# Position terms sent in two halves, local values in three parts, latents batch by batch, contexts normalised early: one change to a fused decoder layer

## What is computed

```
n  = layernorm(x)
x1 = x + local_attention(n)             # 8 heads of 16, blocks of 12 tokens, context 24, a relative
                                        # position term shifted row by row, tanh cap at 50, softmax
x2 = x1 + cross_attention(layernorm(x1), ctx)
                                        # 16 heads of 64, 512 contexts per batch; both inputs get
                                        # their own layernorm inside; rope on the keys;
                                        # clip(q.k/8, -11, 11), softmax; @ Wo + bo
x3 = x2 + routed_mixture(layernorm(x2)) # 12 experts, top 3 of 12, three routers, gelu
```

## Time and profile before

| | |
|---|---|
| median of 3 runs | 504.03 us (503.49 to 505.67) |
| the profiled execution | 503.41 us |
| its span in the profile | 501.7 us |
| mean granted TensorE clock | 0.962 |
| PE busy | 450.8 us (90%) |
| PE weight loads | 327.8 us (65%) |
| DVE busy | 321.8 us (64%) |
| POOL busy | 241.8 us (48%) |
| ACT busy | 187.4 us (37%) |

### The profile page before, as it was taken

The page is one execution under the profiler, slowest core; times in us unless marked ns, Lnnn a source line. Parts: engine busy times, 40 slices in busy tenths (PEclk is TensorE's granted clock), DMA queues, the critical chain, the costliest instruction groups (busy, mean ns, idle before and its releaser), DMA issues.

```text
span 501.7 us, 8554 instructions
## 1 busy us (share of the span) xinstructions
PE 450.8 (90%) x3282; PEld 327.8 (65%) x3282; DVE 321.8 (64%) x686; ACT 187.4 (37%) x290; POOL 241.8 (48%) x209
## 2 busy tenths in 40 slices
PE   2982968988799999999999999588999999999997
PEld 1761746656466676667677667266667777888885
DVE  8952695999976756765769866834463533275454
ACT  5744435454444545543544544112334532300000
POOL 7441344789577776787678748224333333000000
PEclk9997887999899999999999999788999999999999
DMA  7359500000000000000000020010222110000000
GB/s 171 116 104 99 130 2 1 2 0 1 0 1 1 2 1 1 1 1 0 1 2 2 2 87 1 21 43 22 65 63 64 63 64 21 2 6 12 10 5 12
DMA packets 31658, 15.08 MB, mean 30 GB/s; under 512 B 16077, under 2 KB 29314, under 8 KB 31618
## 3 DMA queue, kind: packets, MB, share of 16 engines
q1 hardware_dynamic: 30916, 14.25, 12.3%
q10 hardware_dynamic: 702, 0.28, 0.2%
HBM read 12.56 MB, written 1.97 MB: 29 GB/s over the span
## 4 chain that ended last, share of the span: by engine, by line
PE 70%; DVE 16%; issue 4%; ACT 4%; DMA 3%; POOL 2%; SPq 1%; DVEq 0%; ACTq 0%; POOLq 0%
PE psum L1044 9%; PE psum L1027 9%; PE psum L847 7%; PE psum L1175 5%; PE psum L1212 4%; PE psum L1211 4%; PE psum L1213 4%; PE psum L1177 4%; PE psum L1176 4%; DVE xn L1255 3%; PE psum L1063 3%; PE psum L950 2%; PE psum L1078 2%; PE psum L1054 2%; DVE rden L1428 2%
## 5 line engine op out<-in xcount | busy, mean ns | idle before, releaser
L465 POOL TENSOR_TENSOR e_part<-e_sb 128x512 f32<-128x512 f32 x64 | 91.0, 1439 | 39.8 <-DVE e_sb L1421 39.8
L703 ACT ACTIVATE e_sb<-psum 128x1024 f32<-128x1024 f32 x64 | 62.2, 1023 | 15.6 <-PE psum L1027 15.5
L1027 PE MATMUL psum<-q_t,kT 64*128 64x256 f32 x512 | 64.8, 392 | 0.3 <-ACT e_sb L703 0.3
L1044 PE MATMUL psum<-e_sb,v_sb 128*64 128x256 f32 x512 | 63.7, 392 | 0.0
L497 POOL TENSOR_TENSOR xeT_lo<-xeT,xeT_hi 128x512 fp32r<-128x512 f32 x24 | 30.9, 1290 | 67.0 <-ACT xeT_hi L717 67.0
L1428 DVE RECIPROCAL rden<-psum 128x256 f32<-128x256 f32 x32 | 56.0, 1749 | 2.1 <-PE psum L1054 2.0
L457 POOL TENSOR_TENSOR k_rot<-rope_a,rope_b 128x512 f32<-128x512 f32 x32 | 41.3, 1291 | 32.8 <-DVE rope_b L1317 32.8
L1596 DVE SCALAR_TENSOR_TENSOR x_sb<-psum,dw,x_sb 128x128 f32<-128x128 f32 x96 | 33.7, 351 | 34.8 <-PE psum L1213 32.2
L685 ACT ACTIVATE kT<-psum 128x512 f32<-128x512 f32 x32 | 19.2, 599 | 94.5 <-PE psum L950 94.3
L1027 PEld LDWEIGHTS psum<-q_t,kT 64*128 64x128 f32 x512 | 47.3, 188 | 10.9 <-issue 5.2
L1421 DVE TENSOR_SCALAR e_sb<-e_sb 128x1024 f32<-128x1024 f32 x64 | 47.7, 781 | 7.5 <-ACT e_sb L703 7.5
(11 more groups left out here) (189 smaller groups left out, 793.2 us busy)
## 6 DMA issues: line engine op xcount, KB each, us to landing
w_raw<-in_L_ffn_W_dram SPq DMA_DIRECT2D x24, 256.0 KB, 2.7
ctx_sb<-in_ctx_dram SPq DMA_DIRECT2D x4, 256.0 KB, 5.7
bd_dram<-bd_raw SPq DMA_DIRECT2D x4, 206.2 KB
bd<-bd_dram SPq DMA_DIRECT2D x8, 99.0 KB
vbd<-v_dram SPq DMA_DIRECT2D x8, 79.7 KB
v_dram<-v_tok SPq DMA_DIRECT2D x4, 136.0 KB, 2.2
vbd<-v_dram SPq DMA_DIRECT2D x8, 65.3 KB
raw<-in_L_xattn_Wkv_dram SPq DMA_DIRECT2D x2, 256.0 KB, 5.4
```

Of the source, the lines that this page charges most:

```text
L465: pool.tensor_tensor(e_part[:, p % 2, half, :, :], e_sb[:, i % ERING, :, 0, :], e_sb[:, i % ERING, :, 1, :], ALU.add)\
L703: act.activation(e_sb[:, i % ERING, :, :, :].rearrange("p a k t -> p (a k t)"), psum[:, a:a + 2, :].rearrange("p a b -> p (a b)"), ACT.Exp ...
L1027: mm = pe.matmul(psum[:, 2 * (i % 2) + a, t * S:(t + 1) * S], kT[rows, p % 3, kt * P:(kt + 1) * P], q_t[rows, j % 2, p % 2, :], start=True ...
L1044: mm = pe.matmul(psum[DX * a:DX * a + DX, pv_bank(p), 0:S], v_sb[g % 2][:, kt, 2 * pp + a, :], e_sb[:, i % ERING, a, t, :], start=(kt == 0 ...
```

## The change

It has five parts.

1. **Position terms in two halves.** Chunks 0 to 2 (12 groups) and 3 to 5 (10 groups) are stored and loaded apart, each with semaphores of its own (4 + 4 stores, 8 + 8 loads). The third `relative` and `positions_out` stand ahead of the values; the store of the first half stands ahead of the stores of the values. `add_positions(c)` waits for its half alone.
2. **Values in three parts**: 24 DMAs of 33, 33 and 25 windows in place of 16 of 50 and 41. `local_values(c)` waits for its third.
3. **Contexts early.** On DVE the statistics of context batches 1 to 3 stand between the two halves of `add_positions`, and the normalisation of all three behind the second half, ahead of `local_normalize(0)`. The four last `weight_rest` of POOL stand behind their reciprocal deviations, and the two loads of Wq ahead of the context loads.
4. **Latents batch by batch**, 2 tiles at a time: batch 0 between the chunks of the local attention, batches 1, 2 and 3 in rounds 0 to 3, 6 to 9 and 14 to 17. `output_bias` moves from rounds 0 and 4 to rounds 5 and 18.
5. **The way into the rounds.** `turn_latents(0)` and `queries(0)` stand earlier on PE; one key unit and one `turn_keys` move behind the first scores.

The diff, cut to its core:

```diff
+        def spread_slots(part):
+            def slot(w):
+                return NBP * (w // NB) + w % NB
+            per = CG * WG * NCH // SPREADS
+            return slice(slot(per * part), slot(min(per * (part + 1), WALL) - 1) + 1)
+        def half_groups(half):
+            return slice(CG * HCH * half, min(CG * HCH * (half + 1), NGRP))
         def last_chunk(b):
...
-        LATENT_ROUNDS = (1, 2, 3)
+        LATENT_ROUNDS = {1: (0, 1, 2), 2: (6, 7, 8), 3: (14, 15, 16)}
         CONTEXT_ROUND = {0: 1, PPB - 2: 2, 2 * PPB - 2: 3}
-        extras = {5: ("latents", 1)}
+        extras = {rounds[2] + 1: ("latents", b) for b, rounds in LATENT_ROUNDS.items()}
         for b in range(1, B):
...
-            def spread_values(pair):
-                ns = (slice(0, SPLIT_SLOT), slice(SPLIT_SLOT, NW))[pair]
+            def spread_values(third):
+                ns = spread_slots(third)
                 windows = v_dram.rearrange("(n t) c -> t n c", t=CH)
...
                         sp.dma_start(vbd[part * CH * G + g:(part + 1) * CH * G:G, ns, g, :, :].rearrange("t n h d -> t n (h d)"),
-                                     windows[:, ns.start + part:ns.stop + part, g * 2 * DE:(g + 1) * 2 * DE]).then_inc(s[f"v_spread{pair}"], 16)
+                                     windows[:, ns.start + part:ns.stop + part, g * 2 * DE:(g + 1) * 2 * DE]).then_inc(s[f"v_spread{third}"], 16)
...
               .then_inc(s["v_padded"], 16)
-            for n in range(2, 4):
+            for n in range(2, 6):
                 load_weights(n)
...
+            def store_positions(half):
+                sp.wait_ge(s["bd_raw_done"], HCH * (half + 1))
+                ks = half_groups(half)
+                for i in range(WG):
+                    sp.dma_start(bd_dram[i:WALL:WG][ks].rearrange("k q r -> q k r"), bd_raw[QT * i:QT * i + QW, ks, :])\
+                      .then_inc(s[f"bd_stored{half}"], 16)
+            def shift_positions(half):
+                sp.wait_ge(s[f"bd_stored{half}"], 16 * WG)
+                ks = half_groups(half)
+                for i in range(WG):
+                    shifted = bd_dram[i:WALL:WG][ks].rearrange("k (h c) r -> h k (c r)", h=2)
+                    for h in range(2):
+                        sp.dma_start(bd[QT * i + CH * h:QT * i + CH * (h + 1), ks, :],
+                                     shifted[h, :, 0:CH * GK].rearrange("k (c r) -> c k r", r=GK)).then_inc(s[f"shifted{half}"], 16)
+            store_positions(0)
             sp.wait_ge(s["pad_set"], 3)
...
                              v_tok[:, TPB * b:TPB * (b + 1), :, :].rearrange("p t h e -> p t (h e)")).then_inc(s["v_stored"], 16)
-            sp.wait_ge(s["bd_raw_done"], NCH)
-            for i in range(WG):
-                sp.dma_start(bd_dram[i:WALL:WG].rearrange("k q r -> q k r"), bd_raw[QT * i:QT * i + QW, :, :]).then_inc(s["bd_stored"], 16)
-            sp.wait_ge(s["bd_stored"], 16 * WG)
+            store_positions(1)
             sp.wait_ge(s["consts"], 6)
-            for i in range(WG):
-                shifted = bd_dram[i:WALL:WG].rearrange("k (h c) r -> h k (c r)", h=2)
-                for half in range(2):
-                    sp.dma_start(bd[QT * i + CH * half:QT * i + CH * (half + 1), :, :],
-                                 shifted[half, :, 0:CH * GK].rearrange("k (c r) -> c k r", r=GK)).then_inc(s["shifted"], 16)
+            shift_positions(0)
+            shift_positions(1)
             sp.wait_ge(s["v_padded"], 32)
...
             sp.wait_ge(s["v_zeroed"], 3)
-            spread_values(0)
-            spread_values(1)
-            for n in range(4, 6):
-                load_weights(n)
+            for third in range(SPREADS):
+                spread_values(third)
             sp.dma_start(bo_all[:, :], x_bo.partition_broadcast(P)).then_inc(s["ld_bo"], 16)
...
                 rstd_of(LN_C + KC * b, KC)
-            rstd_of(LN_1, NT // 2)
-            rstd_of(LN_1 + NT // 2, NT // 2)
-            for n in range(4, 6):
+            for n in range(2, 6):
                 weight_rest(n)
+            rstd_of(LN_1, TPB)
+            rstd_of(LN_1 + TPB, TPB)
...
-            for k in range(KC, K_LEAD):
+            for k in range(KC, K_LEAD - 1):
                 key_sum(k)
...
             halves_summed(0)
+            key_sum(K_LEAD - 1)
             for r in range(NPAIR):
-                if r == LATENT_ROUNDS[0]:
-                    rstd_of(LN_1 + NT, NT // 2)
-                if r == LATENT_ROUNDS[1]:
-                    rstd_of(LN_1 + NT + NT // 2, NT // 2)
+                for b, rounds in LATENT_ROUNDS.items():
+                    for part in range(2):
+                        if r == rounds[part]:
+                            rstd_of(LN_1 + (2 * b + part) * TPB, TPB)
                 if r + 1 < NPAIR:
...
-            for c in range(2):
+            for c in range(HCH):
                 positions_out(c)
...
                                bank(2 * j).rearrange("p (n d) -> p n d", d=DA), ACT.Copy).then_inc(s["v_tok_done"], 1)
-            for c in range(2, NCH):
+            for c in range(HCH, NCH):
                 positions_out(c)
...
             outputs_turned(3)
-            outputs_turned(4)
-            outputs_turned(5)
-            weight_hi(4)
-            weight_hi(5)
-            def latents_f(pair):
-                if pair:
-                    act.wait_ge(s["lat_lo_done"], pair)
+            def latents_f(b):
+                if b:
+                    act.wait_ge(s["lat_lo_done"], b)
                 else:
                     act.wait_ge(s["logit_ps"], NCH)
-                act.activation(lat_f[:, :], bank(MISC_BANK if pair else 5), ACT.Identity, scale=affine[:, 0:1], bias=affine[:, 1:2])\
-                   .then_inc(s["misc_read" if pair else "lat_f_done"], 1)
-                if pair:
-                    act.wait_ge(s["misc_read"], MISC_NO["latents", 1] + 1)
+                act.activation(lat_f[:, :], psum[:, MISC_BANK if b else 5, 0:S], ACT.Identity, scale=affine[:, 0:1], bias=affine[:, 1:2])\
+                   .then_inc(s["misc_read" if b else "lat_f_done"], 1)
+                if b:
+                    act.wait_ge(s["misc_read"], MISC_NO["latents", b] + 1)
                 else:
                     act.wait_ge(s["lat_f_done"], 1)
-                act.activation(lat_hi[:, pair * HALF_TOK:(pair + 1) * HALF_TOK], lat_f[:, :], ACT.Copy).then_inc(s["lat_hi_done"], 1)
+                act.activation(lat_hi[:, b * S:(b + 1) * S], lat_f[:, :], ACT.Copy).then_inc(s["lat_hi_done"], 1)
...
-            keys_turned(0)
             act.wait_ge(s["lat_ps"], 1)
             latents_f(0)
+            outputs_turned(4)
+            keys_turned(0)
+            outputs_turned(5)
...
             local_values(5)
+            turn_latents(0, 5, "lat_ps")
             turn_outputs(4)
+            turn_keys(0)
             turn_outputs(5)
             unit(UNITS)
+            queries(0)
             local_project(2)
             local_project(3)
-            turn_keys(0)
-            turn_latents(0, 5, "lat_ps")
             unit(UNITS + 1)
-            queries(0)
-            unit(UNITS + 2)
-            turn_keys(1)
...
             scores(0)
+            turn_keys(1)
+            scores(1)
+            unit(UNITS + 2)
             turn_keys(2)
-            scores(1)
...
                 dve.wait_ge(s["logit_ps"], c + 1)
-                dve.wait_ge(s["shifted"], 16 * 2 * WG)
+                dve.wait_ge(s[f"shifted{c // HCH}"], 16 * 2 * WG)
                 ks = groups(c)
...
                 key_unit(m)
-            for c in range(NCH):
+            for c in range(HCH):
                 add_positions(c)
+            for b in range(1, B):
+                context_statistics(b)
+            for c in range(HCH, NCH):
+                add_positions(c)
+            for b in range(1, B):
+                context_normalize(b)
...
-            def latents(pair, part):
-                before = 2 + B + 2 * pair
-                tiles = range(4 * pair, 4 * pair + 4)
-                lo = LN_1 + pair * NT
+            def latents(b, part):
+                before = 2 + B + 2 * b
+                tiles = range(TPB * b, TPB * (b + 1))
+                lo = LN_1 + 2 * TPB * b
                 if part == 0:
...
                         normalize(xn[:, t, :], x_sb[:, t, :], lo + i).then_inc(s["xn1_done"], 1)
-                    dve.wait_ge(s["xn1_done"], 4 * (pair + 1))
-                    statistics([xn[:, t, :] for t in tiles], lo + 4)
+                    dve.wait_ge(s["xn1_done"], TPB * (b + 1))
+                    statistics([xn[:, t, :] for t in tiles], lo + TPB)
                 else:
...
                     for i, t in enumerate(tiles):
-                        normalize(xn[:, t, :], xn[:, t, :], lo + 4 + i).then_inc(s["lat_in_done"], 1)
+                        normalize(xn[:, t, :], xn[:, t, :], lo + TPB + i).then_inc(s["lat_in_done"], 1)
...
-            def latents_lo(pair):
```

(30 more changed lines are left out.)

35 lines of the change are left out of this document (17 added, 18 removed).

## The result

The change makes the kernel faster: **488.15 us** median (487.66 to 488.99, 4 runs) where the kernel before has 503.76 (502.90 to 505.67); the ratio is 0.9687 with an interval of 0.9656 to 0.9718. Forecast were 493.1 us and a gain of 10.3; measured are 15.6 by the medians and 15.2 between the two profiled spans (501.7 and 486.5 us).

A forecast was written before the change was run, and what follows sets the result against it. DVE, not PE, was taken to bound rounds 0 to 6; before them, PE waits for position terms and latents. Terms -1.4 - 7.0 - 1.7 - 0.2 = -10.3 from 503.4 gave 493.1 us (chance 0.58), range 487.0 to 498.5.

The forecast's parts named there:

- rival A: DVE's wall ahead of the first outputs is thinner (2.5 us better) or rounds hide more latents (489 us); chance 0.18.
- B: Rival: DVE's wall is thicker, second half late or all 12 normalisations blocked; 5 us more, 498; chance 0.13.
- D: Rival: little gain, first stores wait for the queue and latents cost in rounds what they gain; about 502; chance 0.07.
- Position terms and DVE behind it: Ahead of the first outputs: earlier position terms, then DVE late next with 7.2 us of normalisations; turn_outputs(0) 1.4 us earlier.
- at that rate 33, 66 and 91 windows: Spread values: from 50 windows in 4.9 us, parts there at 46.0, 49.3 and 51.7 us.
- Price of an issue: SP queue: 20 more DMAs costed at nothing; 0.6 us per spread issue, so 24 end near 51.
- Rival C: Slower by the price of a DMA: 2.31 us per issue, third part at 93, about 531 us; chance 0.04.
- Latents: First outputs to scores ahead of round 0: half the tiles, PE's idle time and low clock go; -7.0 us.
- Round 0: Round 0 loses the bias, 4.13 us on DVE, and gets 0.65 of statistics; -1.7 us.
- Rounds: Rounds 1 to 6: excess 6.9 us before, 6.7 after, with 2.2 per bias load; -0.2, between -3.5 and +4.
- all latents hidden: The favourable bound of the term for rounds 1 to 6, -3.5 us.
- the sign of being wrong: Spread values landing after 62, or rounds 6 to 9 and 14 to 17 longer than 7.5 us each.

The follow-up runs named there:

- pool_waits: The change, but POOL's four subtractions wait until DVE has done all 12 context normalisations; 0.9683 of the kernel before.
- third_act_pool_waits: The change with the first third of the spread values issued from ACT's queue and POOL's four subtractions behind the 12 normalisations; 0.9662 of the kernel before.
- latents_of_four: The change with the latents of batch 1 ahead of the rounds again, transposes of batch 0 waiting for all four tiles; 0.9771 of the kernel before.
- no_bias: The change without output_bias, so DVE has 8 instructions less in rounds 5 and 18; 0.9647 of the kernel before.
- tile_by_tile: third_act_pool_waits with context batches 2 and 3 normalised one tile a round, and the second bias load one tile a round in rounds 19 to 22; 0.9593, 483.21 us.
- first_third_act: The change, but the first third of the spread values (8 DMAs) is issued from ACT's queue instead of SP's; 0.9754 of the kernel before.

## Why the prediction was right, and where it was off

The sign, the places and the order were right; the gain was a third too small. The time lies inside the range, 1.2 us from its lower end, and it is rival A's (489) and not the forecast's. A had two conditions: a thinner wall of DVE, which did not come (7.02 us), and rounds that hide more, which did, by other work than it named. Of B and D the trace shows nothing: no normalisation was blocked beyond the four, and the first stores went out at 23.18, as soon as ACT had the third chunk out (23.16). By the steps:

*Position terms and DVE behind it, -1.4: measured -1.5, and -3.0 in the second profile.* The adds, the 7.2 us of the normalisations (7.02) and their bound beside an idle POOL (3.4; 3.16 in pool_waits) came out. Its claim that DVE alone is late next was wrong. The values arrived at 47.95 and not at 46.0, because the step "at that rate 33, 66 and 91 windows" took a price per window where the queue has one per issue. That this 2 us error did not move the term is luck: PE's path ended 0.2 us ahead of DVE's. pool_waits shows that freeing DVE alone gives nothing, and third_act_pool_waits that freeing both makes the stage 3.9 us shorter, though little of it reached the end. So A would have won its 2.5 us only with both.

*Price of an issue, nothing: nearly.* Issues took 0.84 us on average and not 0.6, and the last ended at 59.65 and not at 51. The third part landed at 61.37, 0.6 us before it was needed; the second part was 0.63 us late, and the time of the first was set by 8 issues of 0.76 us. Rival C is out: 16 loads were issued in 8.16 us. The Trainium skill (DMA: Bandwidth & Descriptors, Rules for kernel authors) would have transfers under 64 KB coalesced, as mostly overhead. As a reason against this change the runs contradict it: the kernel is faster (0.9687), and with the position terms whole it loses 5.7 us of that; for the values, where two parts do as well as three, they do not. The prediction also has the sizes wrong in one place: the halves of the stores are 112.5 and 93.8 KB, and only the loads and the values are below 64.

*Latents, -7.0: measured -8.4.* latents_of_four confirms the idle time and the clock (5.7 us). The other 2.7 were not tried apart; the new order on PE and ACT, which the prediction put at nothing, is the likely place.

*Round 0, -1.7: measured -1.7.* No run tried it apart, and it rests on the same price of 2.2 us for a load that failed in the next term, so the agreement may be luck.

*Rounds, -0.2: measured -3.6. This is the term that failed*, by the price read off one round: a load of 4.13 us in a round of 9.05, hence an excess of 2.2, and 4.5 for the two halves of the bias. no_bias gives 0.05 + 1.4. The base of 6.82 came from two rounds of 6.46 and 7.18, while PE's own rounds run from 6.3 to 8.3 us, and a long round may only hold work that the next one is spared. The round that was read, in the kernel before, and the next one:

```profile
269.91:278.96 9.05, 8.09 (x61) 5.49 (x61) 8.69 (x11) 4.62 (x7) 6.87 (x7) 1.00 0.01 2
278.96:282.43 3.47, 3.47 (x32) 2.44 (x30) 3.38 (x4) 0.74 (x2) 2.36 (x2) 1.00 0.00 0
```

PE idles for 0.96 us in the two together, so that load cost 1.0 us at most and not 2.2; the columns for PE would have told it. The upper end of that term, -3.5, is called "all latents hidden", but by its own prices (1.5 and 0.7) that gives -2.4. The runs say that it was the bias that was hidden, while the latents cost 0.8 us in rounds 7 to 16, where no other side work changed, and, since rounds 17 to 19 took 21.87 us before and 22.80 in no_bias, 0.9 there. Two rounds also met the sign of being wrong (6 to 9 and 14 to 17 above 7.5 us): round 14 with 8.45 us, which had 8.44 before, and round 17 with 8.22, which had 6.48.

## What to carry to other kernels

Two engines that are each late by the same amount form one gate: an experiment on either shows nothing, and only both together show the gain. Price side work against the sum of several rounds with and without it, or by the idle time that it leaves on the engine that bounds, not by the length of one round. A load is cheap where that engine's own work plus the load fits into the round of the one that bounds, which its busy time in each round shows. Ahead of a gate ask where PE will idle, since the low clock that follows is paid by whatever stands behind it.

## What the runs showed of the hardware

The issue of a spread DMA took 0.76 us at the median with 33 and 25 windows and with 50 and 41; from ACT's queue eight took 6.5 to 7.3 us in five profiles. Ahead of the end of the program, a low stretch of PE's clock lasted 3.41, 6.83 or 10.24 us, and two profiles of one program had 10.24 and 6.83. Each began in or shortly behind idle time of PE: in tile_by_tile at 43.0 us, with PE idle from 40.7 to 42.9, in first_third_act at 52.7, with PE idle from 47.9 to 53.1. And the transfers from ACT's queue did not only use idle DMA time. The stretches of the change and of third_act_pool_waits while the position terms load (the last two figures are the DMA share and GB/s):

```profile
36.00:38.00 2.00, 1.10 (x5) 0.61 (x5) 1.83 (x5) 0.39 (x1) 1.73 (x3) 1.00 0.64 124
```

```profile
36.00:38.00 2.00, 1.54 (x5) 0.97 (x6) 1.37 (x4) 0.60 (x1) 1.81 (x2) 1.00 1.03 133
```

Two queues raise the share from 0.64 to 1.03 and the bytes moved by a fourteenth. From the first issue of the first half's loads to its last landing are 6.5 to 7.6 us in the seven profiles with the halves on one queue, and 7.9 to 9.5 in the five with two. The adds behind them waited in all five of these, from 0.38 us in first_third_act (share 0.85) to 3.10 in tile_by_tile (share 1.03), and in one of the seven, 1.06 us in the change's first profile. Why it varies so among kernels with the same DMAs was not tried.
